# Row maxima of two heads at once in the two halves of TensorE's rows, one visit per key tile

## What is computed

```
x = x + tanh(g_xattn) * attention(layernorm(x), ctx)      # x [32,100,256], ctx [32,1444,256]
  Q, K, V = projections with biases, 16 heads of 16
  scores = Q @ K^T / sqrt(16);  attn = softmax(scores);  out = (attn @ V) @ Wo^T + bo
x = x + tanh(g_ffn) * experts(layernorm(x))
  top 3 of 12 by softmax of router logits; relu(x @ w1[e] + b1[e]) @ w2[e] + b2[e]
  weight of an expert = mean softmax weight of the rows that chose it;
  the sum is scaled by 1 - 0.8 * (phi > 0.7), phi from the mean over the rows
```

## Time and profile before

| | us |
|---|---|
| median of 3 runs | 2209.78 (2208.51 to 2213.41) |
| the profiled execution | 2204.03 |
| its span in the profile | 2202.3 |
| TensorE matmul busy | 2086.9 (95%) |
| VectorE busy | 1480.1 (67%) |
| ScalarE busy | 1305.6 (59%) |
| GpSimd busy | 806.0 (37%) |

### The profile page before, as it was taken

One profiled execution on the slowest core, in us unless ns is written; L12 is line 12 of the kernel. 1 busy time (PEld: TensorE's weight loads), 2 busy tenths in 40 slices (PEclk: granted clock), 3 DMA queues, 4 the chain that ended last, 5 costly groups with the idle time before them and its releaser, 6 DMA issues. The chain is left out here.

```text
span 2202.3 us, 63899 instructions
## 1 busy us (share of the span) xinstructions
PE 2086.9 (95%) x24150; PEld 1848.7 (84%) x24150; DVE 1480.1 (67%) x3330; ACT 1305.6 (59%) x3073; POOL 806.0 (37%) x1187
## 2 busy tenths in 40 slices
PE   5899999999999999999999999999998399999994
PEld 4688888888888888888888888888887299999993
DVE  4777777777777777777777777777774433333334
ACT  1366666656666656666666666666666177777771
POOL 4333344333344333443333433334431133333331
PEclk9999999999999999999999999999999699999996
DMA  5555555555555555555555555555554394333335
GB/s 137 151 132 141 142 145 135 143 137 137 138 134 140 139 141 136 137 135 135 139 139 143 140 138 140 139 137 134 136 129 149 129 313 109 59 59 58 60 52 190
DMA packets 230670, 293.42 MB, mean 133 GB/s; under 512 B 83512, under 2 KB 156188, under 8 KB 230108
## 3 DMA queue, kind: packets, MB, share of 16 engines
q1 hardware_dynamic: 204396, 258.76, 44.2%
q0 software_dynamic: 18528, 21.64, 5.2%
q10 hardware_dynamic: 7440, 8.95, 1.2%
HBM read 104.01 MB, written 42.92 MB: 67 GB/s over the span
## 5 line engine op out<-in xcount | busy, mean ns | idle before, releaser
L641 DVE TENSOR_REDUCE max_part<-max_ps 100x1 f32<-100x512 f32 (+1 forms) x1536 | 994.9, 655 | 353.9 <-PE max_ps L930 324.5
L517 ACT ACTIVATE probs<-score_ps 128x400 f32<-128x400 f32 x1498 | 733.4, 503 | 412.0 <-PE score_ps L913 401.5
L930 PE MATMUL max_ps<-k_stack,q_stack 96*100 96x512 f32 (+1 forms) x1536 | 597.2, 389 | 12.8 <-DVE max_part L641 12.5
L913 PE MATMUL score_ps<-q_stack,k_stack 97*128 97x200 f32 (+1 forms) x2996 | 598.3, 282 | 1.3 <-ACT probs L517 0.5
L913 PEld LDWEIGHTS score_ps<-q_stack,k_stack 97*128 97x128 f32 (+1 forms) x2996 | 463.2, 183 | 66.5 <-issue 30.4
L446 POOL TENSOR_TENSOR ctx_hi<-ctx_raw,zero_col 128x256 fp32r<-128x256 f32 (+1 forms) x384 | 213.3, 586 | 467.8 <-PE v_ps L944 430.7
L981 PE MATMUL pv_ps<-probs,v_ones 128*17 128x100 f32 x12288 | 303.1, 250 | 5.6 <-ACT pv_out L525 2.7
L981 PEld LDWEIGHTS pv_ps<-probs,v_ones 128*17 128x17 f32 x12288 | 256.0, 98 | 51.7 <-issue 37.5
L930 PEld LDWEIGHTS max_ps<-k_stack,q_stack 96*100 96x100 f32 x1536 | 257.1, 167 | 25.4 <-DVE max_part L641 20.3
L451 POOL TENSOR_TENSOR ctx_lo<-ctx_raw,ctx_hi 128x256 fp32r<-128x256 f32 (+1 forms) x384 | 257.2, 700 | 7.5
L566 ACT ACTIVATE k_hl<-k_ps,bk_c 128x512 fp32r<-128x512 f32 (+1 forms) x192 | 127.3, 663 | 215.9 <-PE k_ps L961 193.4
(11 more groups left out here) (197 smaller groups left out, 2528.1 us busy)
## 6 DMA issues: line engine op xcount, KB each, us to landing
k_stack<-k_hl SPq DMA_DIRECT2D x512, 128.0 KB, 2.6
ctx_raw<-in_ctxT SPq DMA_DIRECT2D x64, 512.0 KB, 4.4
k_stack<-k_hl SPq DMA_DIRECT2D x512, 64.0 KB, 2.2
k_stack<-k_hl SPq DMA_DIRECT2D x256, 105.0 KB, 2.4
w_all<-in_w SPq DMA_DIRECT2D x24, 640.0 KB, 9.5
ctx_raw<-in_ctxT SPq DMA_DIRECT2D x32, 420.0 KB, 4.7
k_stack<-k_hl SPq DMA_DIRECT2D x256, 52.5 KB, 2.0
x_t<-rows_by_expert SPq DMA_DIRECT2D x86, 134.5 KB, 2.3
```

What stands on the lines that cost most here:

```text
L517: act.activation(probs[0:tw, n % PROBS, :], score_bank(n)[0:tw, 0:UH * SQ], ACT.Exp, scale=SCALE).then_inc(exp_done, 1)
L641: dve.tensor_reduce(max_part[b % 2][:, h, j:j + 1], max_ps[m % 2][0:SQ, 0:CW[j]], AX.X, ALU.max).then_inc(max_read, 1)
L913: ins = pe.matmul(score_bank(n)[0:TW[i], 2 * SQ * p:2 * SQ * (p + 1)], k_stack[b % 2][:, 2 * u + p, 128 * i:128 * i + TW[i]], q_stack[b % ...
L930: pe.matmul(max_ps[m % 2][0:SQ, 0:CW[j]], q_stack[b % 3][0:96, h // 2, SQ * (h % 2):SQ * (h % 2) + SQ], k_stack[b % 2][0:96, h // 2, k0[j] ...
```

## The change

- **Layout.** `k_stack` and `q_stack` have 128 rows: 64 for each head of a pair, four rows per head column (high and low parts, and in the fourth a plane of ones in `k_stack` against a zero or the negated maximum in `q_stack`). `k_hl` becomes `k_planes` with seven planes; ACT writes the high part twice in one instruction of 1024 columns, and SP moves four planes with one transfer, four transfers of 128 rows per job for eight of 64 and 32 before. The negated maxima go to `q_stack` in four transfers for one; the queries are written to memory in eight transfers for four and read back in two for four.
- **Maxima.** One visit in each slot, at its end: two pairs of matmuls. In a pair the two heads stand in rows 0 to 63 and 64 to 127 and go to two banks. VectorE reduces the four banks with two instructions of 1024 columns, one slot's visit at the start of its next slot.
- **Banks.** `max_ps` has four banks. `v_ps` and `small_ps` are now the first two of them, so V, the small jobs and the second pair of a visit wait for one another: the V copy of ScalarE and the reader of the small job have to be done before the second pair, and the first reduction before V and the small job of the next slot.
- **Order.** TensorE: scores 0, scores 1, K or attention times V, scores 2, small job, all six V matmuls, scores 3, visit. ScalarE: the V copy before the fourth exponential, the K copy behind it. VectorE's low part of K one slot later.
- **Context.** `ctx_hi` and `ctx_lo` are a ring of six tiles; GpSimd splits half a chunk at a time; the K matmuls of the chunk that wraps are cut in two.
- **Beginnings.** VectorE's memsets of `q_stack`, `v_ones` and `pv_ps` come behind the weight split; stages start one slot earlier. In the expert program `w1` and `w2` have semaphores of their own, the transfer of `b2` is started behind the first copies, and the second copy of `w1` behind the first tile's activations.

```diff
-AT_XQ, AT_MAX, AT_NEG, AT_SCORE, AT_PV, AT_POST = -5, 6, 18, 20, 21, 33
+AT_XQ, AT_MAX, AT_NEG, AT_SCORE, AT_PV, AT_POST = -4, 5, 18, 20, 21, 33
-        max_ps = [pb(f"max_ps{i}", [128, 512]) for i in range(2)]
-        v_ps = pb("v_ps", [128, 512])
+        max_ps = pb("max_ps", [128, 4, 512])
+        v_ps, small_ps = max_ps[:, 0, :], max_ps[:, 1, :]
...
+        def stack_keys(eng, b, j, o):
+            for q in range(4):
+                dst = k_stack[b % 2][:, 4 * o + q, k0[j]:k0[j] + CW[j]].bitcast(F32)
+                src = k_planes[32 * q:32 * q + 32, 3 * o:3 * o + 4, 0:CW[j]].bitcast(F32)
+                eng.dma_start(dst, src).then_inc(k_stacked[j][o], 16)
...
+                wait(pool, v_done, tile + 2 - RING)
...
-                            act.activation(k_hl[:, o, 1, 0:CW[j]], k_ps[:, 0:CW[j]], ACT.Identity,
+                            act.activation(k_planes[:, 3 * o + 1:3 * o + 3, 0:CW[j]],
+                                           k_ps[:, 0:CW[j]].unsqueeze(1).broadcast_to([128, 2, CW[j]]), ACT.Identity,
...
-                dve.tensor_reduce(max_part[b % 2][:, h, j:j + 1], max_ps[m % 2][0:SQ, 0:CW[j]], AX.X,
-                                  ALU.max).then_inc(max_read, 1)
+                for two in range(2):
+                    dve.tensor_reduce(max_part[b % 2][:, :, 2 * (s % TPC) + two, j],
+                                      max_ps[0:SQ, 2 * two:2 * two + 2, 0:CW[j]], AX.X,
+                                      ALU.max).then_inc(max_read, 1)
...
-                wait(pe, max_read, m + 1 - 2)
-                pe.matmul(max_ps[m % 2][0:SQ, 0:CW[j]],
-                          q_stack[b % 3][0:96, h // 2, SQ * (h % 2):SQ * (h % 2) + SQ],
-                          k_stack[b % 2][0:96, h // 2, k0[j]:k0[j] + CW[j]],
-                          start=True, stop=True).then_inc(max_done, 1)
+                wait(pe, max_read, 2 * visits_before(g))
+                for two in (1, 0):
+                    if two == 0:
+                        wait(pe, v_read, min(g + 1, NT * B))
+                        wait(pe, small_read, jobs_until(g))
+                    pair = 2 * (s % TPC) + two
+                    for e in range(2):
+                        half = slice(64 * e, 64 * e + 64)
+                        ins = pe.matmul(max_ps[0:SQ, 2 * two + e, 0:CW[j]],
+                                        q_stack[b % 3][half, pair, SQ * e:SQ * e + SQ],
+                                        k_stack[b % 2][half, pair, k0[j]:k0[j] + CW[j]], start=True, stop=True)
+                ins.then_inc(max_done, 1)
...
+                wait(pe, max_read, 2 * visits_before(g) - 1)
...
             for g in range(FIRST, LAST):
                 scores(g, 0)
-                maxes(g, 0)
-                values(g, 0)
...
                 scores(g, 1)
-                maxes(g, 1)
                 keys_of(g)
                 times_v(g)
                 scores(g, 2)
-                maxes(g, 2)
-                values(g, 1)
+                for kind, b in small_jobs(g):
+                    small_job(g, kind, b)
+                values(g)
                 scores(g, 3)
-                maxes(g, 3)
+                maxes(g)
```

More of the change, by code:

```diff
@@ L79, in small_jobs @@
     jobs = [(kind, batch_at(g, at)) for at, kind in SMALL.items() if batch_at(g, at) is not None]
-    jobs.sort(key=lambda job: job[0] != "nm")
     return jobs + [("const", 0)] * (g == CONST_SLOT)
@@ L89, with jobs_until, visits_before @@
 SMALL_NO = {job: n for n, job in enumerate(job for g in range(FIRST, LAST) for job in small_jobs(g))}
+def jobs_until(g):
+    return sum(len(small_jobs(s)) for s in range(FIRST, g + 1))
+def visits_before(g):
+    return min(max(g - AT_MAX, 0), NT * B)
 def wait(eng, sem, value):
@@ L190, in attention @@
         x_res = sb("x_res", [SQ, D])
-        x1 = sb("x1", [SQ, D])
-        heads = x1
+        x1, heads = x_res, x_in
         stats2 = sb("stats2", [SQ, 6])
@@ L464, in _ @@
                 for j in range(NC):
-                    b = batch_at(g, 4 * j - 4)
-                    if b is not None:
-                        split(NC * b + j)
+                    for h in range(2):
+                        b = batch_at(g, 4 * j + 2 * h - 4)
+                        if b is not None:
+                            split(NC * b + j, h)
                 if g == FIRST + 1:
@@ L608, in link @@
                 dve.wait_ge(setup, own[0])
-            dve.memset(pv_ps[:], 0.0).then_inc(setup, 1)
-            for p in range(3):
-                dve.memset(q_stack[p][:].bitcast(F32), 0.0).then_inc(setup, 1)
-            dve.memset(x_row[:], 0.0).then_inc(setup, 1)
-            dve.memset(small[:], 0.0).then_inc(setup, 1)
-            own[0] += 6
-            dve.wait_ge(setup, own[0])
             dve.wait_ge(kv_in, 32)
@@ L1126, in experts @@
         x_in = [sem(f"x_in{p}") for p in range(AHEAD)]
-        w_in = [sem(f"w_in{e}") for e in range(NE)]
+        w1_in = [sem(f"w1_in{e}") for e in range(NE)]
+        w2_in = [sem(f"w2_in{e}") for e in range(NE)]
         w1_ready = sem("w1_ready")
```

340 lines of the change are left out of this document (178 added, 162 removed).

## The result

The changed kernel takes **2366.89 us** (median; 2361.08 to 2368.24) against 2210.18 us of the kernel before on the same chip: a ratio of 1.0701, 95% interval 1.0684 to 1.0717. I had forecast 2187 us, range 2150 to 2268. It is 7% slower, and outside the range.

The account below looks back on a forecast made before the run. TensorE's own stream was taken to set the time. -0.5 us per batch over 30 batches (-15), with the beginnings -23, gave 2181 us for the profiled execution and 2187 us for the median; range 2150 to 2268.

Parts of the forecast that it names:

- Transfers: SP's K transfers and negated maxima: fewer, larger transfers, with more than a slot in hand, would cost nothing.
- The sum per batch: Visit, waits, K matmuls and small jobs together (-0.4 - 0.4 + 0.1 + 0.2): -0.5 us per batch.
- The visit: TensorE's four maxima per slot: 0.86 us, 0.82 with 420 columns, second pair waiting for the V copy; gain 0.4 per batch.
- The waits that go: TensorE's idle time before maxima, nearly all for VectorE's reductions, would vanish: -0.4 us per batch.
- K: K matmuls of the wrapping chunk, 12 x 0.12 for 6 x 0.23 twice per batch: +0.1 us per batch.
- The rival of the switch: Switching TensorE to row halves costs like column groups, 0.20 us per slot on the way out: 2259 us; chance 0.33.
- The doubt that 96 rows are not a half: Maxima of 96 rows showed no switch cost behind full-row loads, but may not tell about halves of rows.
- The rival of halves in series: The two heads' maxima in row halves run one after another on TensorE, +1.0 us per batch: 2217 us; chance 0.10.
- second pair released by ScalarE's V copy in nearly every slot: Expected sign in TensorE's waits: the visit's second pair waits for the V copy, 0.2 us or less each.
- the case of a late ScalarE: ScalarE slips 0.2 us per slot in the mean, from jobs ahead of the V copy: 2230 to 2290 us; chance 0.10.
- The beginnings: Start of the pipeline: later memsets, half a context chunk and fewer K transfers bring first scores 7 us earlier (0 to 12).
- The expert program: Separate weight semaphores in the expert program would save 1 us.

Follow-up runs that it names:

- e2: Changed kernel with the context load started one slot earlier on SP, ahead of the negated maxima and K transfers: 2194.10 us, ratio 1.0001.
- e8: Kernel before with only the load of the next context chunk started two slots later: 2533.31 us, ratio 1.1515.
- e3: Changed kernel with both edits, GpSimd's scatters and counts one slot later and context load one slot earlier and first on SP: 2194.68 us, ratio 0.9999.
- e7: Kernel before, unchanged, run once more as a single execution for a profile: 2193.61 us.
- e4: e3 with all four maxima over full 128 rows, one after another, in place of halves: 2203.73 us, ratio 1.0040.
- e11: e6 with the expert program's first loads and weight copies as in the kernel before: 2144.40 us, ratio 0.9778.
- e6: e2 with the next slot's first score pair ahead of the visit and attention times V right behind it: 2144.80 us, ratio 0.9771.
- e9: e6 with maxima over full 128 rows in place of halves: 2200.43 us, ratio 1.0026.
- e1: Changed kernel with GpSimd's counts and three scatters one slot later, behind the second half of the split: 2386.08 us, ratio 1.0882.

## Why the prediction failed

**The step that failed is "Transfers ... Both have more than a slot in hand: nothing."** I priced the K transfers and the negated maxima by their own landing and their own readers, and asked of no other transfer what stands ahead of it on SP. The context load stands behind both, and in the rows above it starts 8.85 us after its buffer is free. Of the load itself I noted only that half a chunk suffices for V; that the buffer is now free two slots later, and the load written two slots later, was in the diff (4j - 3 to 4j - 1) and in none of my terms. The repeated kernel before waits mostly for TensorE's V matmuls in its split (435.2 us, against 32.8 for the load): its load was written three slots ahead of its split, that of the changed kernel one. e2 alone brings the ratio from 1.070 to 1.0001; e8 takes as little as this one lateness to make the kernel before 15% slower. Each ratio is against the kernel before on its own chip. That is the loss shown from both sides: taken away by this edit alone, and brought about by it alone.

**GpSimd's order**, with the scatters between the two halves of a split, was missing from the working too. It adds 4.1 us to the loop of one chunk in three; e3 shows that it costs nothing once the load is in time.

**The sum per batch** was forecast at -0.5 us. With the load in time the mean over 31 steps is 0.0 (51.21 for 51.22 in e7), but the steps differ: the 29 in the middle take 51.47 for 51.60, -0.13 each, and the first takes 50.1 for 46.7. The terms, from e2 and e3:
- *The visit*: 0.86 and 0.82 us forecast. With its switches it takes 0.95 (0.10 + 0.75 + 0.10) and 0.90, so the visit alone is not -0.4 but +0.6 per batch.
- *The waits that go*: more than the 0.4 I took. Grouping the starts of 20 batches by what runs, scores, maxima and V matmuls together take 0.02 us per slot less in e2 than in e7, 0.2 per batch, so that 0.8 went elsewhere. The way into the block is no part of it: with full rows (e4) the two score pairs ahead of the block take 0.52 for twice 0.20, so the scores pay there what the maxima of before paid (0.33 at 648.46 in the earlier trace rows). I did not separate the rest.
- *K* costs 0.1 to 0.2 for the 0.1 of the forecast.

**The rival of the switch** had the mechanism right and its size: 0.20 us per slot, though as 0.10 in and 0.10 out. With the load in time the ratio is 1.0001, though, and not the 1.022 that this rival comes to. Where it was wrong is the balance: I added it to a visit of 0.86 that already held 0.11 for the exposed load. The doubt that 96 rows are not a half was sound; I then put the forecast against it. The rival of halves in series falls: the second matmul of a pair starts with the first, and four maxima take 0.65 where they would take 0.94. The 0.08 that I took for the second head was right in size, but it lies in the length of the pair and not between the two starts. The sign "second pair released by ScalarE's V copy in nearly every slot, 0.2 us or less each" held (280 waits in 1200 us, 0.19 each, in e2), and the case of a late ScalarE did not come as a slip of 0.2 us per slot, though weight loads of scores wait for exponentials more often (58.0 us in 255 waits for 13.5 in 46).

**The beginnings**: first scores forecast 7 us earlier. First K and first maxima came early, the scores did not; PE's timeline of the changed kernel, then the source views of scores and maxima in e2 and three lines of its timeline, show it:

```profile
27.93 0.55 PE L1000 MATMUL k_ps<-ctx_hi,w_hi 128*128 128x256 f32 x1 [4.23 <-POOL ctx_lo L469]
...
79.32 0.55 PE L1000 MATMUL k_ps<-ctx_hi,w_hi 128*128 128x256 f32 x1 [4.50 <-POOL ctx_lo L469]
...
L938 PE MATMUL score_ps<-q_stack,k_stack x3016: 250/275/536, 92.3 to 1706.1; 128*128 128x200 f32 x189
L962 PE MATMUL max_ps<-k_stack,q_stack x1536: 343/468/750, 34.9 to 1667.9; 64*100 64x512 f32 x128, 64*100 64x420 f32 x64
...
61.48 0.78 PE L962 MATMUL max_ps<-k_stack,q_stack 64*100 64x512 f32 x4 [0.16 <-DVE max_part L656]
63.62 0.36 PE L980 MATMUL max_ps<-w_hi,ctx_hi 128*128 128x256 f32 x1 [1.36 <-issue]
64.71 0.79 PE L962 MATMUL max_ps<-k_stack,q_stack 64*100 64x512 f32 x4 [0.15 <-DVE max_part L656]
```

In the changed kernel two waits for the split are 8.7 us (first scores at 99.7). In e2 the first maxima start at 34.9 and the first scores at 92.3; in the kernel before (e7) 42.3 and 91.6. Of 7.4 us gained, 8.1 are lost in between: with no scores to do, the V matmuls of a slot wait 1.2 to 1.4 us (the reductions of a whole visit lie behind it), and visits follow each other at 3.2 to 3.3 us. I had named this limit and set no price on it. The first step of 50.1 for 46.7 us, behind the first transpose, takes another 3.4 back.

**The expert program**: -1 us forecast. From the last transpose to the end e2 takes 519.7 us and e7 517.0, but the stretch varies from 517.9 to 528.1 among versions with the same start, and e11 is no faster than e6. The term is neither shown nor refuted.

## What to carry to other kernels

A buffer that is loaded, used and loaded again is a loop: add up the free buffer's wait on the issuing queue, the landing, the work on it and what stands between, and compare the sum with the period, before and after any edit that moves one of them. A small wait in the profile before says that there is slack, not how much of it an edit may use. In this kernel partial rows of TensorE pay where the second pair is ready when the first has streamed, and most where the work next to them is in a part of the array as well (0.27 us per visit beside the block, 0.10 elsewhere).

## What the runs showed of the hardware

- Going to halves of rows costs 0.10 us and going back to full rows 0.10; from halves to the block's groups of 17 columns no cost showed (0.65 us for a visit ahead of the block and 0.64 ahead of scores, e6), while from full rows it was 0.08 (1.02 against 0.94, e9).
- Two heads in two halves, writing different banks, stream together: they start within 0.01 us of each other, and four maxima of 512 columns take 0.65 us and of 420 0.56, against 0.94 and 0.77 in series.
- The stall of 3.5 us before 1072.51 costs more than itself. TensorE is idle throughout 1070 to 1072; the first K matmuls behind it still stand 0.23 us apart, as at 2.4 GHz, then 0.30 and 0.43, which is 512 columns at 1.2 GHz. From 1074 to 1076 us the granted clock is 0.50 (1.2 GHz), and by 1077 it is 1.00 again. PE's timeline of the changed kernel, then the window with the columns of the earlier trace rows:

```profile
1073.28 0.51 PE L1000 MATMUL k_ps<-ctx_hi,w_hi 128*128 128x512 f32 x1
1073.58 0.63 PE L1000 MATMUL k_ps<-ctx_lo,w_hi 128*128 128x512 f32 x1
1074.01 0.63 PE L1000 MATMUL k_ps<-ctx_hi,w_lo 128*128 128x512 f32 x1
...
1074.00:1076.00 2.00, 2.00 (x10) 1.76 (x9) 0.00 (x0) 0.73 (x2) 0.00 (x0) 0.50 0.44 109
```

- A K transfer of 128 rows and 256 KB takes SP about 1.0 us to issue (4.14 for four), where one of 64 or 32 rows mostly took 0.6; runs of eight took 9.01 and 12.98 us in e2. It lands in 4.7 us for 2.6. Once the load stood ahead, TensorE waited for K transfers 3.6 us in all (e2).
- Open: in about half the batches of the changed kernel ScalarE and VectorE both start an operation some 2 us after TensorE has released it, just as GpSimd issues its scatters (the exponential at 1012.28 after 3.16 us idle, the reciprocal at 1012.99 put down to "remote", scatters from 1009.47 to 1013.09). In e1, e2 and e3 the scatters take as long and the reciprocal's idle time is 0.6 us in every batch but the last two. e1 still has the late load, so it takes both, the late load and the scatters at this place. I have no cause for it.
